# Graph-network kernel, first layer: a gathered batch's landing is waited for after the next batch's gathers are issued

## The reference, cut to what matters

```python
# x: (100000, 256) f32; src, dst: 25000 edges sorted by dst; edge_weight: (25000,)
deg = maximum(segment_sum(ones, dst), 1.0);  s = deg ** -0.5
h = maximum(layernorm(x), 0)
x = x + s * segment_sum((s * h)[dst] * edge_weight[:, None], src)     # layer 0
h = maximum(layernorm(x), 0)
x_i, x_j = h[dst], h[src]
m = relu(concat([x_i, x_j - x_i]) @ W1 + b1) @ W2 + b2
x = x + segment_sum(m, dst) / (count(dst) + 1e-8)                     # layer 1
```

## Time and profile before

| what | us |
|---|---|
| median of 3 runs | 2122.19 |
| lowest and highest run | 2121.31 and 2128.58 |
| the profiled execution, its own time | 2127.77 |
| its span in the trace | 2125.6 |
| granted TensorE clock over the span | 0.912 of full speed |
| busy: PE, DVE, ACT, POOL | 1685.9, 1470.8, 1006.6, 1272.0 |
| first gather of layer 0 | at 130.32 |
| first scatter of layer 0 | at 469.96 |
| first gather of layer 1 | at 1003.67 |

### The profile page before, as it was taken

One profiled execution on the slowest core, in us unless ns is written; L12 is line 12 of the kernel. 1 busy time (PEld: TensorE's weight loads), 2 busy tenths in 40 slices (PEclk: granted clock), 3 DMA queues, 4 the chain that ended last, 5 costly groups with the idle time before them and its releaser, 6 DMA issues.

```text
span 2125.6 us, 46204 instructions
## 1 busy us (share of the span) xinstructions
PE 1685.9 (79%) x13740; PEld 1478.3 (70%) x13740; DVE 1470.8 (69%) x5883; ACT 1006.6 (47%) x2064; POOL 1272.0 (60%) x1004
## 2 busy tenths in 40 slices
PE   4958788788855565650499999999999999999991
PEld 1237777678855554640389888888888888888881
DVE  6968898889965655640377777777766767777660
ACT  0014444445433232320366766667665656656561
POOL 2013333358878878875444333378888888888854
PEclk9979999999988787775699999999999999999996
DMA  7989999846665655654999999965555555555543
GB/s 242 317 290 322 323 324 332 276 101 109 111 103 91 98 94 97 98 72 72 333 328 330 336 331 331 335 143 97 95 93 92 98 91 98 92 92 97 93 65 39
DMA packets 140467, 376.43 MB, mean 177 GB/s; under 512 B 31391, under 2 KB 95656, under 8 KB 127528
## 3 DMA queue, kind: packets, MB, share of 16 engines
q0 software_dynamic: 84672, 128.51, 34.3%
q1 hardware_dynamic: 27452, 208.63, 27.6%
q10 hardware_dynamic: 28304, 38.85, 7.0%
HBM read 323.36 MB, written 258.12 MB: 274 GB/s over the span
## 4 chain that ended last, share of the span: by engine, by line
POOL 22%; DMA 13%; issue 12%; SPq 5%; ACT 0%; DVE 0%; POOLq 0%; ACTq 0%
POOL table_out L951 12%; DMA table_out<-x 11%; POOL ends L939 10%; SPq L926 5%; DMA table_out<-e_ring,e_targets_all 2%; ACT ends L1162 0%; DMA ends<-x,keys 0%; DVE e_moments L1013 0%; SPq L922 0%; ACT hid L1176 0%; DVE feat_lo L1080 0%; ACT feat_hi L1169 0%; ACT hid_hi L1179 0%; ACT e_ring L1194 0%; POOLq L949 0%
## 5 line engine op out<-in xcount | busy, mean ns | idle before, releaser
L939 POOL DMA_INDIRECT ends<-x,keys x392 | 398.9, 1018 | 309.5 <-PE ps_h L1263 107.4
L468 POOL DMA_INDIRECT x<-slots,targets_all x196 | 327.7, 1672 | 87.6 <-issue 56.4
L951 POOL DMA_INDIRECT table_out<-e_ring,e_targets_all x196 | 321.5, 1640 | 92.0 <-issue 55.8
L788 PE MATMUL ps_deg<-table,hot 128*128 128x128 bf16 x5488 | 329.5, 222 | 52.0 <-issue 26.5
L788 PEld LDWEIGHTS ps_deg<-table,hot 128*128 128x128 bf16 x5488 | 315.9, 99 | 61.5 <-issue 48.6
L453 POOL DMA_INDIRECT slots<-in_x,row_idx x196 | 210.2, 1072 | 239.7 <-DMA slots<-in_x,row_idx 170.2
L802 PE MATMUL ps_sum<-msg_hi,same 128*128 128x260 f32 x784 | 158.7, 334 | 207.1 <-issue 200.4
L1263 PE MATMUL ps_h<-feat_hi,w_hi 128*128 128x512 f32 x784 | 314.5, 401 | 10.4 <-DVE feat_lo L1080 5.3
L1263 PE MATMUL ps_h<-feat_lo,w_hi 128*128 128x512 f32 x784 | 310.3, 396 | 0.0
L1263 PE MATMUL ps_h<-feat_hi,w_lo 128*128 128x512 f32 x784 | 310.3, 396 | 0.0
L802 PEld LDWEIGHTS ps_sum<-msg_hi,same 128*128 128x128 f32 x784 | 135.2, 237 | 213.2 <-issue 213.2
(11 more groups left out here) (141 smaller groups left out, 3420.4 us busy)
## 6 DMA issues: line engine op xcount, KB each, us to landing
table_out<-x SPq DMA_DIRECT2D x400, 252.0 KB
x<-in_x SPq DMA_DIRECT2D x400, 250.0 KB
hi_row<-hi_rows ACTq DMA_DIRECT2D x49, 256.0 KB
src_row<-src_rows ACTq DMA_DIRECT2D x49, 256.0 KB
dst_row<-dst_rows ACTq DMA_DIRECT2D x49, 256.0 KB
ends<-x,keys POOLq DMA_INDIRECT x392
slots<-in_x,row_idx POOLq DMA_INDIRECT x196
x<-slots,targets_all POOLq DMA_INDIRECT x196
```

Of the source, the lines that this page charges most:

```text
L468: pool.indirect_dma_start(out=x1_d, out_offset=bass.IndirectOffsetOnAxis(ap=targets_all[:, b, j:j + 1], axis=0), in_=slots[:, b % SLOTS, j ...
L788: last = nc.tensor.matmul(ps_deg[q][k][:, j * P:(j + 1) * P], hot[:, c, k, j * P:(j + 1) * P], table[:, c, part, :], start=(c == 0 and par ...
L939: pool.indirect_dma_start(out=ends[b % NE][:, n, :], out_offset=None, in_=x1_d, in_offset=bass.IndirectOffsetOnAxis(ap=keys[:, 1 - end, at ...
L951: pool.indirect_dma_start(out=out, out_offset=bass.IndirectOffsetOnAxis(ap=e_targets_all[:, b, j:j + 1], axis=0), in_=e_ring[:, b % RING1, ...
```

## The change

It leaves out the wait for the batch just issued and puts in its place the wait for the batch before it. Batch 27, the last of the first part, is then waited for in step 0 of the second part, after the four scatters of batch 0. No gather, scatter or semaphore is added or removed, and the order of the DMAs on POOL stays.

```diff
@@ the first part: batches 0 to LEAD0 - 1 @@
                     for j in range(W):
                         gather(b, j)
-                    gathered(b)
+                    if b > 0:
+
+                        gathered(b - 1)
 
                 for k in range(FLIGHT):
                     pool.wait_ge(bulk[k], 16 * ROUNDS)
...
                 left = W * (NB - LEAD0)
-                ready = LEAD0
+                ready = LEAD0 - 1
                 for b in range(NB):
                     first, last = min(left, 2 * b // 1), min(left, 2 * (b + 1) // 1)
                     scatter(b)
+                    if b == 0:
+                        gathered(ready)
+                        ready += 1
                     while ready < LEAD0 + first // W:
 
                         gathered(ready)
```

## The result

The changed kernel takes **2073.1 us** (median of 4 runs, 2069.62 to 2074.15) against 2124.55 us for the kernel before on the same chips (4 runs, 2121.31 to 2128.58). The ratio is 0.9759, with a 95% interval of 0.9736 to 0.9782: 51 us, 2.4%, less. The forecast was 2085.5 us, in a range of 2073 to 2097; the measured time lies inside that range by 0.1 us, so the mechanism has to be read with care.

A forecast was written before the change was run, and what follows sets the result against it. The prediction took layer 0 to be bound by POOL's 49 steps, starting at the first scatter. That scatter 40.5 us earlier, less 4 us given back, saves 36.5 us from 2122.19: 2085.5 us, range 2073 to 2097.

The forecast's parts named there:

- What bounds layer 0: Layer 0 ends where POOL's 49 steps end; they begin at 469.96 us, the number the change can move.
- Step (1): First part of layer 0: overlapping landing waits with the next issue cuts 13.4 us a batch to 7.5.
- packet turns: Rival, 9%: gather packets take turns with the copy's large pieces, pace 11.2 us a batch, 2096 us.
- nothing comes of it: Rival, 4%: POOL is held in issuing beyond four open gathers, pace stays near 13.4 us, 2122 us.
- Step (2): From batch 16 on, gathers also wait for DVE's statistics of batch b - 16; this costs nothing.
- Step (3): First bulk copy: seven more batches beside it, 1.77 us each, move its end from 415 to about 429 us.
- Step (4): Start of the second part: first scatter 0.5 us after the copy, at 429.5 us, 40.5 us earlier.
- Step (5): Second part of layer 0: compute runs longer at full rate beside the scatters, lengthening steps; 4 us given back.
- Step (6): Layer 1, behind the barrier, is shifted whole; its own length changes by 0 us.
- the copy pays nothing: Rival, 6%: gathers go into gaps, the first copy still ends at 415 to 418 us, 2073 us in all.
- The slower rival: Rival, 3%: dense gathers delay the copy by more than their bytes, over 7.9 us per moved batch; 2135 us.
- the free copy: Rival, 6%: the first copy is not delayed by the added gathers; gain 49 us, 2073 us.

## Why the prediction was right, and where not

- **What bounds layer 0** (POOL's 49 steps, which begin when the gathers and the copy are both through): right, by the table above.
- **Step (1), the pace**: 6.8 us a batch against 7.5 forecast, and 13.4 before. Since batch 27 had 95 us to spare, the miss cost nothing. The rival *packet turns* (11.2 us, from the rule that the Trainium skill gives in "DMA: Bandwidth & Descriptors", section "Queues, rings and completion order") is not what happened; the trace does not speak against turns, but against each small packet standing behind a whole 0.71 us piece. The rival *nothing comes of it* falls too: gathers are issued at 1.25 us intervals with eight open.
- **Step (2), the throttle**: right, no wait on DVE's statistics up to 412 us; one batch further ahead it does bind.
- **Step (3), the copy: this is the term that was mis-sized.** It was given 14 us and got -4, an error of 18 to 19 us in the copy's end, which also lies outside the 415 to 433 that the step took as its bounds. About 8 us are the price: 7 x 0.87 = 6.1 us and not 14. The price came from the share of the DMA engines that gather packets held (12.9%), as if that share were taken from others. The DMA queues of 150 to 318 us show that it was not, first the kernel before, then the kernel before in its second execution, then the changed kernel:

```profile
DMA packets 12527, 54.56 MB, mean 325 GB/s; under 512 B 3794, under 2 KB 6866, under 8 KB 9912
...
q1 hardware_dynamic: 5209, 41.72, 68.6%
...
q0 software_dynamic: 2462, 6.71, 13.7%
```

```profile
DMA packets 12629, 55.95 MB, mean 333 GB/s; under 512 B 3875, under 2 KB 6902, under 8 KB 9916
...
q1 hardware_dynamic: 5409, 43.31, 71.0%
...
q0 software_dynamic: 2413, 6.58, 13.3%
```

```profile
DMA packets 14534, 59.60 MB, mean 355 GB/s; under 512 B 4472, under 2 KB 7421, under 8 KB 11985
...
q1 hardware_dynamic: 5080, 40.68, 62.9%
q0 software_dynamic: 4736, 12.93, 24.0%
```

  Shares near 1.0 looked like full engines, and yet 6.22 MB more of gathers went through for 1.04 MB less of the copy, while the mean packet of q1 shrank from 0.686 x 2688 / 5209 = 0.354 us to 0.333 us. So a packet's time holds waiting as well as work; what it waits for these rows don't show. Against the first execution a batch would cost (1.04 / 41.72 x 168) / (6.22 / 0.524) = 0.35 us, but that is the one whose copy was late. Against the second, 6.35 MB more of gathers stand beside 2.63 MB less of the copy: 10.2 us for 12.1 batches, **0.84 us each**, which agrees with the 0.87 from the copy's ends. The 1.59 MB between the two executions of one kernel are 6 of the 7 us by which their copies end apart. That the memory sets the price is an argument and was not tested: a gather reads the HBM once, the copy reads and writes it, and 0.524 MB at twice the copy's own 317 GB/s would be 0.83 us, close to 0.87. The other 10 us or so are the base: the shown execution of the kernel before ended its copy at 414.1, where two others with 21 batches beside it show 404.5 and 406.9. The forecast took one execution's copy end as the kernel's. The old kernel hid that spread, the new one is bound by it.
- **Step (4)**: 0.5 us from the copy's end to the first scatter was too little. From the start of the last piece to the first scatter it is 2.0 to 3.3 us in the seven executions where the copy ends last (3.2 in the changed kernel), and 1.6 us to the first gather where seven batches were held back.
- **Step (5)**: 3.1 us given back against 4 forecast, in one pair of executions. Over all of them the second part takes 534.1 us on average with the first scatter at 405 to 414 (five), and 531.7 where it is at 444 or later (five), so 2.4 us: the right sign and size, though single ones lie 5 us apart. DVE's waits for rows are 11 now instead of 16, so they begin at batch 38, as forecast (37 or 38), and the steps take 11.1 us up to there (245.2 / 22) and 10.8 after it (215.9 / 20).
- **Step (6)**: right, 0.5 us.
- The case *the copy pays nothing* (2073 us, 6%) gave the measured number for a reason that is not the measured one: the copy does pay 6 us for seven batches. The slower rival needed 7.9 us a batch and is off by a factor of nine.
- **The number.** In the profiled executions the gain was 54.0 us and not 36.5; of the 17.5 us between them 16.2 are the first scatter, steps (3) and (4). That the time lies in the range at all is partly luck: its lower bound was set by the case of the free copy, and the base was taken from a median of 2122.19 that came out as 2124.55 with one more run.

## What to carry to other kernels

Where one queue does both issue and waiting, find the two conditions that a later stage waits for and see by how much each is late: here one wait for landings, harmless in each step, put 55 us between the end of a copy and the first use of it. Once it is gone, the other condition is the bound, so its spread from run to run and its price for shared traffic have to be measured, not read from one execution; a busy share of the DMA engines near 1.0 doesn't mean that bytes added there push out as many others (here 6.35 MB added pushed out 2.63 MB of the copy). And an instruction taken out from in front of a wait saves only what it is longer than the wait that it hid.

## What the runs showed of the hardware that was not expected

- Rows gathered into SBUF beside an HBM to HBM copy cost the copy about 0.87 us per 0.524 MB (0.84 by the bytes moved, 0.46 if its latest end is the base), packed or strewn, while the total rate rose from 325 or 333, in two executions, to 355 GB/s.
- A gather of 131 KB, one open at a time, takes 7.1 us from issue to landing beside the copy and 3.2 us without it, yet beside the copy eight open ones pass at 6.8 us per four.
- The end of a 400-piece copy differed by 7 us between two executions of the same program (414.1 and 406.9).
